# Five turns on TensorE issued between the filling products and the value products of their head

## The reference

```python
scale, shift = split(emb @ W_emb + b_emb)
xn = rms_norm(x, g_norm) * (1.0 + scale) + shift
q, k, v = heads(xn @ W_qkv)                      # 16 heads of width 32
q, k = rms_norm(q, g_q), rms_norm(k, g_k)
attn = softmax(einsum('bhqd,bhkd->bhqk', q, k) * d ** (-0.5))
o = einsum('bhqk,bhkd->bhqd', attn, v)
a = o + o @ W_out
h = gelu(bitlinear(a, w_fc))                     # 512 -> 2048
out = x + bitlinear(h, w_proj)                   # 2048 -> 512, layer_norm of h first
```

## Time and profile before

| | us |
|---|---|
| median of 3 runs | 1103.45 (1103.19 to 1105.78) |
| the profiled execution | 1104.76 |
| its span, first to last instruction | 1102.9 |
| PE busy | 1059.3 (96%) |
| DVE busy | 857.8 (78%) |
| ACT busy | 804.2 (73%) |
| POOL busy | 557.2 (51%) |
| granted TensorE clock, mean | 0.981 |

### The profile page before, as it was taken

One profiled execution on the slowest core, in us unless ns is written; L12 is line 12 of the kernel. 1 busy time (PEld: TensorE's weight loads), 2 busy tenths in 40 slices (PEclk: granted clock), 3 DMA queues, 4 the chain that ended last, 5 costly groups with the idle time before them and its releaser, 6 DMA issues.

```text
span 1102.9 us, 24517 instructions
## 1 busy us (share of the span) xinstructions
PE 1059.3 (96%) x9521; PEld 672.7 (61%) x9521; DVE 857.8 (78%) x1615; ACT 804.2 (73%) x1370; POOL 557.2 (51%) x367
## 2 busy tenths in 40 slices
PE   8668899999999999999999999999999999999998
PEld 2234666656666665766666576666657666665666
DVE  4778769787877978788796878879687887868657
ACT  4867686868778686877868687786858677584854
POOL 1842290835638093653809265381927448192613
PEclk9869899999999999999999999999999999999999
DMA  9910303231121313112131312213131211212100
GB/s 345 339 33 21 90 13 78 64 78 59 29 74 44 87 54 78 59 36 68 44 97 44 78 59 44 59 45 96 45 78 59 51 55 42 58 40 59 59 18 23
DMA packets 79667, 77.14 MB, mean 70 GB/s; under 512 B 8640, under 2 KB 60224, under 8 KB 79040
## 3 DMA queue, kind: packets, MB, share of 16 engines
q1 hardware_dynamic: 79520, 75.57, 24.9%
q10 hardware_dynamic: 32, 0.01, 0.0%
HBM read 41.85 MB, written 8.40 MB: 46 GB/s over the span
## 4 chain that ended last, share of the span: by engine, by line
PE 88%; DVE 4%; ACT 3%; issue 1%; POOL 1%; DMA 1%; SPq 1%; DVEq 0%; ACTq 0%
PE F L954 10%; PE F L955 10%; PE F L800 9%; PE F L802 9%; PE QA L730 3%; PE QA L731 3%; PE QA L732 3%; PE QB L730 3%; PE QB L731 3%; PE QB L732 3%; PE T L1034 3%; PE SB L859 2%; PE SA L859 2%; PE PV L876 2%; PE PV L875 2%; PE PV L874 2%
## 5 line engine op out<-in xcount | busy, mean ns | idle before, releaser
L954 PE MATMUL F<-yT_hi,fc_t 128*128 128x256 f16 (+1 forms) x1040 | 228.3, 272 | 1.1 <-DVE yT_lo L1367 1.1
L955 PE MATMUL F<-yT_lo,fc_t 128*128 128x256 f16 (+1 forms) x1040 | 227.9, 272 | 0.0
L680 POOL TENSOR_TENSOR rqk<-ssq,half 128x16 f32<-128x16 f32 x64 | 193.7, 3033 | 47.3 <-DVE ssq L1545 47.3
L800 PE MATMUL F<-proj_t,hs 128*128 128x512 f16 (+1 forms) x512 | 192.2, 377 | 0.0
L802 PE MATMUL F<-proj_t,hs 128*128 128x512 f16 (+1 forms) x512 | 191.9, 376 | 0.0
L649 POOL TENSOR_TENSOR acc<-acc,hg 128x512 f32<-128x512 f32 x96 | 149.9, 1562 | 14.5 <-ACT hg L1164 1.5
L1506 DVE SCALAR_TENSOR_TENSOR hs<-hg,g_inv,hs 128x512 f16<-128x512 f32 x128 | 106.5, 833 | 62.3 <-ACT hs L1169 62.2
L649 POOL TENSOR_TENSOR acc<-hg 128x512 f32<-128x512 f32 x16 | 20.3, 1267 | 209.7 <-ACT hg L1164 183.1
L656 POOL TENSOR_TENSOR acc<-acc,hq 128x512 f32<-128x512 f32 x90 | 114.1, 1267 | 13.7 <-ACT hq L1235 5.5
L1164 ACT ACTIVATE hg<-F,g_fc 128x512 f32<-128x512 f32 x128 | 87.2, 682 | 44.6 <-PE F L955 44.6
L643 POOL TENSOR_TENSOR rs<-var,half 128x1 f32<-128x1 f32 x32 | 17.6, 550 | 201.2 <-DVE var L1356 201.2
(11 more groups left out here) (252 smaller groups left out, 2742.8 us busy)
## 6 DMA issues: line engine op xcount, KB each, us to landing
stk<-qkT SPq DMA_DIRECT2D x128, 128.0 KB, 2.4
xtok<-in_x SPq DMA_DIRECT2D x17, 512.0 KB, 3.8
xT_sb<-in_xT SPq DMA_DIRECT2D x16, 512.0 KB, 3.6
stk<-qkT SPq DMA_DIRECT2D x128, 64.0 KB, 2.1
xres<-in_x SPq DMA_DIRECT2D x15, 512.0 KB, 3.6
out<-xres SPq DMA_DIRECT2D x15, 512.0 KB, 2.8
stk<-in_w_emb SPq DMA_DIRECT2D x4, 512.0 KB, 6.7
fc_t<-in_w_qkv SPq DMA_DIRECT2D x2, 1024.0 KB, 11.0
```

What stands on the lines that cost most here:

```text
L680: pool.tensor_tensor(rqk[:, n % 2, :], ssq[:, n % 2, :], half[:, :], ALU.pow).then_inc(rqk_r, 1)
L800: pe.matmul(dst, hs[:, 0, k // 2, col:col + P], proj_t[:, k, cols], start=(k == 0), stop=False)
L954: pe.matmul(dst, w, yT_hi[:, k, cols], start=(k == 0), stop=False)
L955: mm = pe.matmul(dst, w, yT_lo[:, k, cols], start=False, stop=(k == KT - 1))
```

## The change

Of the block that follows the filling products in a slot, the piece turn and the stats turn now stand ahead of the value products (and, in iteration 0, of the column sums); the rms and heads turns stay behind them. No instruction is added or taken away, no wait is changed, and the other four engines' lists are the same as before.

```diff
                     for item in filler(i, h):
                         between(item)
-                    if att is not None and h >= BEHIND:
-                        values(h - BEHIND)
-                    if last(att) and h == HEADS - 1:
-                        keep_busy(SB[0], 2)
-                    if isinstance(i, int) and i == 0 and h in COLSUM_AT:
-                        column_sums(COLSUM_AT[h])
                     kind, n = turn_at(i).get(h, (None, 0))
                     if kind == "piece" and qkv is not None:
                         pe.wait_ge(qkn_r, nth(qkv, 4, n + 1))
...
                         mm.then_inc(turned, 1)
+                    if kind == "stats" and ffn is not None:
+                        pe.wait_ge(fold_r, nth(ffn, 1, 1))
+                        open_turn(("stats", 0))
...
+                        mm.then_inc(turned, 1)
+                    if att is not None and h >= BEHIND:
+                        values(h - BEHIND)
+                    if last(att) and h == HEADS - 1:
+                        keep_busy(SB[0], 2)
+                    if isinstance(i, int) and i == 0 and h in COLSUM_AT:
+                        column_sums(COLSUM_AT[h])
                     if kind == "rms" and pre is not None and early(pre):
...
                     if kind == "heads" and att is not None:
                         heads_turn(n)
-                    if kind == "stats" and ffn is not None:
...
```

More of the change, by code:

```diff
@@ L1035, in iteration @@
                         mm.then_inc(turned, 1)
+                    if kind == "stats" and ffn is not None:
+                        pe.wait_ge(fold_r, nth(ffn, 1, 1))
+                        open_turn(("stats", 0))
+                        for s in range(2):
+                            for t in range(TT):
+                                mm = pe.matmul(T[:, s * TT + t:s * TT + t + 1], accf[:, s, t * P:(t + 1) * P],
+                                               ones[:, 0:1], start=True, stop=True)
+                        mm.then_inc(turned, 1)
[5 more added lines that the diff above has]
+                        column_sums(COLSUM_AT[h])
                     if kind == "rms" and pre is not None and early(pre):
```

## The result

The changed kernel takes 1118.55 us (median of 4 runs, 1118.23 to 1118.91), the kernel before, run beside it, 1104.37 (4 runs, 1103.19 to 1105.78). The ratio is 1.0131, with a 95% interval from 1.0119 to 1.0143: 14.2 us slower. The forecast was 11.1 us slower, and its range ended at 1117.5, 14.05 above the 1103.45 that it started from; the time lies outside it, if by little. The profiled execution took 1118.23 us with a span of 1116.3, against 1104.76 and 1102.9.

The account below looks back on a forecast made before the run. TensorE, busy 96% of the span, was taken as the bound, so only its waits count. 0.70 us per iteration times 14 (9.8) plus 1.3 for iteration 0 made 11.1 us: 1103.45 to 1114.5 us, range 1108 to 1117.5.

Parts of the forecast that it names:

- Slot 11: Iterations 1 to 14: turn stays at T's release, TensorE waits 0.51 instead of 0.21 us; cost 0.30 us.
- Slot 12: Iterations 1 to 14: TensorE reaches the turn at the same time, waits 0.12 us for T as before; no cost.
- An exchange: Slot 12: head 9's value products come in between the two turns, head 10's go out, so TensorE's arrival is unchanged.
- Slots 4 and 7: Slot 4 saves 0.04 us, slot 7 waits 0.10 less 0.04; 0.01 to 0.02 us per iteration counted as gain.
- Slot 13: Late value products hold `rden`, then `p_lo` and slot 15's scores; shift per iteration grows to 0.71 us.
- the walk: Slot 13 to iteration's end: turn, value products, `rden`, `o_sb`, `p_lo`, slot 15's scores, fourth `o_sb`, heads turn; shift 0.71 us.
- Iteration 0: Turns put ahead of value products and column sums; mainly 1.2 us more work behind slot 14's turn; 1.3 us taken.
- Cheaper turns: Rival: fp32 weight loads hide behind filling products, 0.24 us saved per iteration, 3.4 in all, time 1100.1; chance 0.05.
- the 5.7 us: Within the cheaper-turns rival: page estimate over 14 iterations if all five turns saved a 107 ns load beyond 0.025 us.
- More than the sum: Rival: late VectorE delays the last `v_lo`; second wait at next iteration's head adds 0.2 us, 1117.3 in all; chance 0.06.

Follow-up runs that it names:

- slot13_only: Against the kernel before, from iteration 1 on the piece turn of slot 13 alone goes ahead of the value products: 1108.4 us (1.0042 of before).

## Why the prediction was off

**Direction and mechanism: right.** A turn that stands ahead of value products waits longer for T, and the kernel gets slower by over 1%.

**Slot 11: right in the changed kernel.** Forecast: the turn does not move against L1384's end and 0.30 us of cover are gone. The turn stands 0.15 behind it, and the scores of slot 12 come 0.76 behind the turn's start instead of 0.47, 0.29 later.

**Slot 12: right number, incomplete reason.** It costs nothing beside slot 11, and 0.30 alone. "An exchange" held only for a TensorE already late. The chain through T should have been priced as one.

**Slots 4 and 7: right.** Slot 4 saved 0.04 and slot 7 cost some 0.09 (forecast: 0.06), of which slot 11's wait took 0.08; 0.03 us per iteration came through instead of the 0.01 to 0.02 taken.

**Slot 13: right up to the end of the walk.** `rden` came as late as said (560.25, against 559.32 + 0.93 by the forecast's steps), and the scores of slot 15 waited for `p_lo`. The step that failed is "In the timeline VectorE has no idle time from 550.17 until the fourth `o_sb`, so its 0.71 us are still there then". 0.09 of them were given back. The rows of before show where the queue was not full, in slot 15:

```profile
553.87 0.60 ACT L1186 ACTIVATE p_hi<-SB 128x512 f16<-128x512 f32 x1
...
554.50 0.69 DVE L1523 TENSOR_TENSOR p_lo<-SB,p_hi 128x512 f16<-128x512 f32 x1
...
554.67 0.38 ACT L1248 ACTIVATE oT_hi<-T 128x256 f16<-128x256 f32 x1 [0.20 <-PE T L884]
...
555.11 0.41 DVE L1384 TENSOR_TENSOR oT_lo<-T,oT_hi 128x256 f16<-128x256 f32 x1
```

`p_lo` of head 15 starts 0.03 behind the end of ScalarE's `p_hi` (554.47), and `oT_lo` 0.06 behind that of `oT_hi` (555.05): VectorE was held for ScalarE at both, too shortly for a bracket. A VectorE that comes late no longer waits there, which gives back 0.03 to 0.04 at the first and 0.04 just behind the second. With 0.61 less 0.03 an iteration costs 0.58, not 0.70, and 14 of them 8.1, not 9.8.

**Iteration 0: wrong, and the reason the range was missed.** The term was 1.3 us with bounds of 0.3 and 1.6, and it measured 4.8 us in the trace of the changed kernel and 5.1 by itself. Its order was priced about right: with the clock held up by the added products it costs 1.7 us in the trace and 1.9 by the median, little over the bound, and 1.2 of the 1.7 lie behind slot 14's turn, as forecast. The steps that failed are two. First, the work that goes behind the waits was priced at the speed that it has in rows 10, so the clock was put at nothing, without a reason; behind the waits of 3.15 and 2.62 us it ran at half the clock, and that is some 3 us. Second, and through the first, "What slots 5 and 8 lose (0.3, and up to 1.2) is swallowed by waits that come later, the one of 2.0 us above all": slot 8 lost 3.0 by the time of slot 11's turn.

That slot 8's turn would wait for so long was hidden in the trace of before, and by the clock again. Rows 11 have no wait for it, since that execution ran at half the clock until 86 us and TensorE came late by itself. In the trace of slot13_only, whose iteration 0 has the same order and which ran there at the full clock, the turn waits behind its value products and column sums too:

```profile
85.45 0.66 PE L1035 MATMUL T<-ident,qkn 128*128 128x128 f32 x4 [1.79 <-DVE qkn L1561]
```

Put ahead of the 1.2 us of work, it waits about that much longer, 3.15.

**The rivals.** "Cheaper turns" has 0.035 to 0.04 us per iteration to show, in slot 4. A turn behind a filling product takes 0.44 us where it took 0.48 in rows 6 (559.32 to 559.76), and the statistics turn gains nothing. So for the fp32 weight loads the trace stays with the rows, far from the 5.7 us that was estimated from the Trainium skill ("TensorE: Matmul & The Clock Gate"; that the fast weight load is not for fp32 stands in Weight-path perf modes, the time of a load in LDWEIGHTS). "More than the sum" came nearest with 1117.3, by luck: no second wait at the head of an iteration appeared, and the iterations cost less than the forecast, not more.

## What to carry to other kernels

Work ahead of a waiting instruction is cover, and its worth is what the queue loses when it is taken away: price a wait by when the awaited thing is ready, not by the wait that the trace shows, which can be nothing because of the cover. If several instructions wait in turn for one buffer, they are one chain that is paid once, so moving one of them alone costs other than its share of moving all. And work moved behind a long wait may run at half the clock, as it did here behind 3.15 and 2.62 us, so look at the first iteration apart: it had over a third of the loss here. A stretch that the trace of before ran at half the clock can hide a wait that other executions have; a second trace shows it.

## What was not expected of the hardware

A standstill of TensorE of 3.15 us was followed by a granted clock of 0.52 over 86 to 92 us, and one of 2.62 us by a mean of 0.76 over 105 to 112; the 1.79 us of slot 8 in slot13_only was not (1.00 over 86 to 92 us), nor was the 0.44 us of slot 11 in each iteration (1.00 over 130 to 1000 us of the changed kernel). Twelve products without use, 2.77 us, in the first of these waits and as many in the second made the kernel faster, 1106.08 against 1109.18 us.

Whether the clock falls at that place differs between executions even without the change. The profiled one of before ran at half the clock for the whole of 80 to 86 us, that of slot13_only, whose iteration 0 is the same, at the full one:

```profile
80.00:86.00 6.00, 5.27 (x38) 2.92 (x39) 5.30 (x8) 4.08 (x6) 3.38 (x1) 0.50 0.01 3
```

```profile
80.00:86.00 6.00, 4.18 (x45) 2.56 (x45) 5.56 (x9) 4.93 (x7) 2.32 (x1) 1.00 0.01 3
```

That the spread of 3 us between the runs of before comes from this was not tried.
